# Attention scores from strips of queries and masked keys, without key transfers, in a fused attention and GRU kernel

## What is computed

```python
# x: [128, 32, 256], cond: [128, 256], 16 heads of 16 features
scale, shift = split(cond @ W_emb + b_emb)
xn = rms_norm(x, g_norm) * (1 + scale) + shift
q, k, v = split(xn @ W_qkv)                  # per head
q, k = rms_norm(q, g_q), rms_norm(k, g_k)
attn = softmax(q @ k.T * 16 ** -0.5)         # within one sequence
o = attn @ v
x = x + o + o @ W_out
# GRU cell, for t in range(32), state h starts as cond
gi, gh = x[:, t] @ W_ih + b_ih, h @ W_hh + b_hh
r, z = sigmoid(gi_r + gh_r), sigmoid(gi_z + gh_z)
n = tanh(gi_n + r * gh_n)
h = (1 - z) * n + z * h
x[:, t] = x[:, t] + h
```

## Time and profile before

| what | us |
|---|---|
| median of 3 runs | 341.93 |
| lowest and highest | 341.85, 342.36 |
| span of the profiled execution, first to last instruction | 340.0 |
| TensorE busy in it | 323.3 |
| VectorE, ScalarE, GpSimd busy | 246.3, 238.0, 224.5 |

### The profile page before, as it was taken

The page is one execution under the profiler, slowest core; times in us unless marked ns, Lnnn a source line. Parts: engine busy times, 40 slices in busy tenths (PEclk is TensorE's granted clock), DMA queues, the critical chain, the costliest instruction groups (busy, mean ns, idle before and its releaser), DMA issues.

```text
span 340.0 us, 12168 instructions
## 1 busy us (share of the span) xinstructions
PE 323.3 (95%) x4177; PEld 293.4 (86%) x4177; DVE 246.3 (72%) x665; ACT 238.0 (70%) x722; POOL 224.5 (66%) x404
## 2 busy tenths in 40 slices
PE   8988899899999999999986999999999999999994
PEld 8767788788888888888874999999999999999994
DVE  3778898888999999999996455565555556555555
ACT  4787777778888788889656566666666666666662
POOL 6787787867777877878778346555555555555542
PEclk9999999999999999999999999999999999999999
DMA  5965237742343333233332221111112111122221
GB/s 202 307 193 151 86 76 234 226 132 85 109 121 113 101 114 99 86 117 116 112 109 65 80 77 48 61 49 62 62 62 62 48 58 50 62 62 62 63 62 33
DMA packets 32205, 34.14 MB, mean 100 GB/s; under 512 B 5286, under 2 KB 26796, under 8 KB 32172
## 3 DMA queue, kind: packets, MB, share of 16 engines
q1 hardware_dynamic: 25868, 26.10, 25.6%
q10 hardware_dynamic: 6304, 7.61, 7.0%
HBM read 12.46 MB, written 8.39 MB: 61 GB/s over the span
## 4 chain that ended last, share of the span: by engine, by line
PE 78%; POOL 7%; SPq 4%; DMA 4%; issue 3%; DVE 3%; ACT 1%; POOLq 0%; DVEq 0%; ACTq 0%
PE bank L1287 38%; PE bank L1244 19%; PE bank L1400 4%; PE bank L1419 4%; PE bank L1388 4%; DMA operands<-operands 4%; PE bank L1531 3%; SPq L414 2%; POOL operands L485 2%; PE bank L1380 2%; SPq L405 2%; PE bank L1250 2%; PE bank L1371 2%; POOL xn L496 1%; POOL xn_lo L531 1%
## 5 line engine op out<-in xcount | busy, mean ns | idle before, releaser
L1287 PE MATMUL bank<-wih_lo,wo_parts 128*128 128x256 f32 x192 | 56.2, 294 | 0.0
L1287 PE MATMUL bank<-wih_hi,wo_parts 128*128 128x256 f32 x192 | 54.6, 285 | 0.2 <-POOL pair_lo L600 0.2
L1287 PE MATMUL bank<-wih_hi,pair_lo 128*128 128x256 f32 x192 | 52.8, 279 | 0.0
L1287 PE MATMUL bank<-wqkv_hi,hT_hi 128*128 128x256 f32 x192 | 52.5, 292 | 0.0
L611 POOL TENSOR_TENSOR operands<-operands,h 128x128 f32<-128x128 f32 x64 | 29.6, 462 | 34.2 <-ACT operands L932 33.4
L1287 PE MATMUL bank<-wqkv_lo,hT_hi 128*128 128x256 f32 x192 | 49.9, 279 | 0.0
L1187 DVE TENSOR_TENSOR operands<-bank,operands 128x128 f32<-128x128 f32 x64 | 18.6, 291 | 39.3 <-ACT operands L929 39.3
L1244 PE MATMUL bank<-wqkv_hi,xn_hi 128*128 128x512 f32 (+1 forms) x124 | 46.4, 375 | 0.2 <-POOL xn_lo L531 0.2
L618 POOL TENSOR_TENSOR w_emb_sb<-h,w_emb_sb 128x256 f32<-128x256 f32 x31 | 22.9, 737 | 30.7 <-DVE h L1204 30.7
L1287 PE MATMUL bank<-wqkv_hi,hT_lo 128*128 128x256 f32 x192 | 42.7, 279 | 0.0
L1244 PE MATMUL bank<-wqkv_hi,xn_lo 128*128 128x512 f32 (+1 forms) x124 | 41.9, 338 | 0.0
(11 more groups left out here) (138 smaller groups left out, 975.2 us busy)
## 6 DMA issues: line engine op xcount, KB each, us to landing
v_diag<-v_rows SPq DMA_DIRECT2D x124, 34.0 KB, 2.1
operands<-operands SPq DMA_DIRECT2D x32, 128.0 KB, 2.1
out_dram<-x ACTq DMA_DIRECT2D x16, 256.0 KB, 2.6
w_emb_sb<-out_dram SPq DMA_DIRECT2D x32, 128.0 KB, 2.1
operands<-operands SPq DMA_DIRECT2D x63, 64.0 KB, 2.0
out_dram<-w_emb_sb SPq DMA_DIRECT2D x31, 128.0 KB, 1.7
x_in<-in_x_dram SPq DMA_DIRECT2D x7, 512.0 KB, 8.6
stage_w<-in_L_cond_W_ih_dram ACTq DMA_DIRECT2D x2, 384.0 KB, 3.4
```

The source lines that it names most:

```text
L1287: return pe.matmul(dst, moved, gate_columns(weights, k, block), start=False, stop=True, skip_group_check=True)
```

## The change

The zeros move from the keys to the queries. ScalarE now copies the keys alone (`kT`, 256 columns) and writes the queries twice with a scale per partition (`strip_parity`), which is one for the partitions of every other strip and zero for the rest (`q_strips`, two copies of 256 columns). A product takes 64 partitions of one of these copies as weights and streams the two masked keys of one sequence, 64 columns; there are 32 of them for a group. The scores read `k_masked` directly: `k_diag`, its memset and its transfers are gone, and with them the helpers by which ScalarE's queue took a share of the transfers. With the transfer gone the scores and all that follows have a lag one smaller (`PE_S` 7 to 6 and so on, `POOL_KEYS` stays at 6), GpSimd does `mask_keys` before `shift`, and the extra work of the last turns stands one turn earlier in the program where it is tied to the pipeline's end, on GpSimd for example.

```diff
-PE_X2T, PE_V, PE_S, PE_PV, PE_QKT, PE_OUT, PE_XT, PE_QK = 11, 4, 7, 8, 5, 10, 2, 3
-ACT_LN, ACT_V, ACT_X2T, ACT_QKT, ACT_EXP, ACT_SQX, ACT_SQK, ACT_OT, ACT_XN, ACT_XHAT = 1, 4, 11, 5, 7, 0, 3, 9, 2, 1
-DVE_QKN, DVE_SS, DVE_OT, DVE_MAX, DVE_RCP, DVE_XMOD, DVE_RES, DVE_O, DVE_PT = 4, 3, 8, 6, 7, 1, 9, 7, 6
-POOL_XN, POOL_KEYS, POOL_OT, POOL_XLO, POOL_NEWTON = 3, 6, 10, 3, 1
-SP_V, SP_KEYS = 5, 6
+PE_X2T, PE_V, PE_S, PE_PV, PE_QKT, PE_OUT, PE_XT, PE_QK = 10, 4, 6, 7, 5, 9, 2, 3
+ACT_LN, ACT_V, ACT_X2T, ACT_QKT, ACT_EXP, ACT_SQX, ACT_SQK, ACT_OT, ACT_XN, ACT_XHAT = 1, 4, 10, 5, 6, 0, 3, 8, 2, 1
+DVE_QKN, DVE_SS, DVE_OT, DVE_MAX, DVE_RCP, DVE_XMOD, DVE_RES, DVE_O, DVE_PT = 4, 3, 7, 5, 6, 1, 8, 6, 5
+POOL_XN, POOL_KEYS, POOL_OT, POOL_XLO, POOL_NEWTON = 3, 6, 9, 3, 1
+SP_V = 5
...
             def place_values(v, slot):
                 sp.wait_ge(v_ready, v + 1)
-                for b in range(2 if isinstance(v, int) and v in SHARED_VALUES else GB):
+                for b in range(GB):
...
-            def place_keys(g, slot):
-                sp.wait_ge(k_masked_ready, g + 1)
-                strips = KEY_STRIPS[:-1] if isinstance(g, int) and g == NG - 1 else KEY_STRIPS
-                for i, (first, count) in enumerate(strips):
-                    rows = slice(PB * first, PB * (first + count))
-                    sp.dma_start(k_diag[rows, slot, i % 2, :, :, :].rearrange("p r j k -> p (r j k)"),
-                                 k_masked[rows, slot, :, :].rearrange("p r f -> p (r f)"))\
-                      .then_inc(k_diag_ready[slot], 16)
...
             def mask_keys(k, slot):
-                pool.wait_ge(qkT_ready, k + 1)
+                pool.wait_ge(kT_ready, k + 1)
                 if later(k, 2):
-                    pool.wait_ge(k_diag_ready[slot], spread(k - 2, slot, len(KEY_STRIPS)))
+                    pool.wait_ge(s_ps, k - 1)
...
             def body(base, u):
+                k = group(base, u, POOL_KEYS)
+                if k is not None:
+                    mask_keys(k, (u - POOL_KEYS) % 2)
                 g = group(base, u, POOL_XN)
                 if g is not None:
                     shift(g, (u - POOL_XN) % 2)
-                k = group(base, u, POOL_KEYS)
-                if k is not None:
-                    mask_keys(k, (u - POOL_KEYS) % 2)
...
-                if turn_is(base, u, NG + 5):
+                if turn_is(base, u, NG + 4):
                     summed_biases()
                 for i in range(2 * KC):
-                    if turn_is(base, u, NG + (1, 5, 6, 6)[i]):
+                    if turn_is(base, u, NG + (1, 4, 5, 5)[i]):
                         gate_weights(i // 2, i % 2)
-                    if turn_is(base, u, NG + (5, 6, 7, 7)[i]):
+                    if turn_is(base, u, NG + (4, 5, 6, 6)[i]):
                         state_weights(i // 2, i % 2)
...
-                act.copy(qkT[:, slot, :], p_qkT[:, :]).then_inc(qkT_ready, 1)
+                act.copy(kT[:, slot, :], p_qkT[:, D:2 * D]).then_inc(kT_ready, 1)
+                if isinstance(g, int) and g == 0:
+                    act.wait_ge(parity_step, 4)
+                for n in range(2):
+                    last = act.activation(q_strips[:, slot, n, :], p_qkT[:, 0:D], ACT.Copy,
+                                          scale=strip_parity[:, n:n + 1])
+                last.then_inc(q_strips_ready, 1)
...
-            dve.memset(operands[:, 0:KD], 0.0).then_inc(k_diag_clear, 1)
...
+            dve.tensor_reduce(strip_rows[:, :], head_rows[:, :].rearrange("p (s r) -> p s r", r=2),
+                              AX_X, ALU.add).then_inc(parity_step, 1)
+            dve.wait_ge(parity_step, 3)
+            dve.tensor_reduce(strip_parity[:, :], strip_rows[:, :].rearrange("p (i n) -> p n i", n=2),
+                              AX_X, ALU.add).then_inc(parity_step, 1)
...
             def scores(g, slot):
-                pe.wait_ge(k_diag_ready[slot], spread(g, slot, len(KEY_STRIPS)))
+                pe.wait_ge(k_masked_ready, g + 1)
+                pe.wait_ge(q_strips_ready, g + 1)
...
                 for c in range(KC):
-                    for b in range(GB):
-                        for i in range(2):
-                            rows = slice(2 * PB * i, 2 * PB * i + 2 * PB)
-                            last = pe.matmul(s_tiles[i][T * b:T * b + T, c * P:c * P + P]
-                                             .rearrange("p (r n k) -> p n r k", r=2, k=T),
-                                             qkT[rows, slot, c * P + T * b:c * P + T * b + T],
-                                             k_diag[rows, slot, :, :, GB * c + b, :], start=True, stop=True)
+                    for n in range(2):
+                        for b in range(GB):
+                            tokens = slice(c * P + T * b, c * P + T * b + T)
+                            columns = slice((2 * c + n) * 2 * T, (2 * c + n) * 2 * T + 2 * T)
+                            for i in range(2):
+                                rows = slice(2 * PB * i, 2 * PB * i + 2 * PB)
+                                last = pe.matmul(s_tiles[i][T * b:T * b + T, columns].rearrange("p (r k) -> p r k", r=2),
+                                                 q_strips[rows, slot, n, tokens], k_masked[rows, slot, :, tokens],
+                                                 start=True, stop=True)
```

More of the change, by code:

```diff
@@ L50 @@
 GATE_LOADS = 11
-LATE_RESULTS = range(24, 28)
-LAST_TURNS = range(34, 39)
-SHARED_VALUES = (3, 4)
+LATE_RESULTS = range(25, 29)
+LAST_TURNS = range(33, 38)
 FIRST_SPREAD = 7
@@ L126, in adaptive_attention_gru @@
         qkn = sb("qkn", [P, 2, 2 * D])
[L127 to L134, removed]
+        kT = sb("kT", [P, 2, D])
+        q_strips = sb("q_strips", [P, 2, 2, D])
+        strip_parity = sb("strip_parity", [P, 2])
+        strip_rows = sb("strip_rows", [P, NB])
+        operands = sb("operands", [P, 6 * D])
+        k_masked = operands[:, 0:2 * 2 * D].rearrange("p (s r f) -> p s r f", s=2, r=2)
         v_rows = sb("v_rows", [P, 4, HEADS, VW])
@@ L239, in adaptive_attention_gru @@
         qkT_ps = sem("qkT_ps")
-        qkT_ready = sem("qkT_ready")
+        kT_ready = sem("kT_ready")
+        q_strips_ready = sem("q_strips_ready")
         k_masked_ready = sem("k_masked_ready")
-        k_diag_ready = [sem("k_diag_ready0"), sem("k_diag_ready1")]
         scores_clear = sem("scores_clear")
@@ L407, in place_values @@
                       .then_inc(v_diag_ready[slot], 16)
-            def place_keys(g, slot):
-                sp.wait_ge(k_masked_ready, g + 1)
-                strips = KEY_STRIPS[:-1] if isinstance(g, int) and g == NG - 1 else KEY_STRIPS
-                for i, (first, count) in enumerate(strips):
-                    rows = slice(PB * first, PB * (first + count))
-                    sp.dma_start(k_diag[rows, slot, i % 2, :, :, :].rearrange("p r j k -> p (r j k)"),
-                                 k_masked[rows, slot, :, :].rearrange("p r f -> p (r f)"))\
-                      .then_inc(k_diag_ready[slot], 16)
-            def body(base, u):
[L419 to L426, removed]
+            def body(base, u):
                 v = group(base, u, SP_V)
-                if v is not None and not (isinstance(v, int) and (v <= 2 or v >= NG - 3)):
+                if v is not None:
                     place_values(v, (u - SP_V) % 4)
[L430 to L433, removed]
+                if turn_is(base, u, SP_V + 2):
                     load_x(4 * FIRST_SPREAD, NG, x_loaded[FIRST_SPREAD])
-            pipeline(sp, body, NG - 1 + max(SP_V, SP_KEYS))
+            pipeline(sp, body, NG - 1 + SP_V)
             for stored in x2_stored:
@@ L485, in mask_keys @@
                 pool.tensor_tensor(k_masked[:, slot, :, :],
-                                   qkT[:, slot, D:2 * D].unsqueeze(1).broadcast_to([P, 2, D]),
+                                   kT[:, slot, :].unsqueeze(1).broadcast_to([P, 2, D]),
                                    gqk_parity[:, :].unsqueeze(2).broadcast_to([P, 2, D]),
@@ L692, in load_gate_weights @@
                 act.dma_start(staged[:, i % KC, :], source[(i % KC) * P:(i % KC) * P + P, :]).then_inc(loaded[i % KC], 16)
[L694 to L704, removed]
-                first, count = KEY_STRIPS[-1]
-                rows, slot = slice(PB * first, PB * (first + count)), (NG - 1) % 2
-                act.dma_start(k_diag[rows, slot, (len(KEY_STRIPS) - 1) % 2, :, :, :].rearrange("p r j k -> p (r j k)"),
-                              k_masked[rows, slot, :, :].rearrange("p r f -> p (r f)")).then_inc(k_diag_ready[slot], 16)
             def gate_weights(c):
@@ L897, in body @@
                     first_state()
-                for v in SHARED_VALUES:
-                    if turn_is(base, u, v + ACT_V):
-                        place_values(v, 2, GB)
                 for i in range(4):
@@ L1415, in attention_products @@
                         head = HC * c + 2 * j + e
```

(2 more changed lines are left out.)

17 lines of the change are left out of this document (5 added, 12 removed).

## The result

The changed kernel takes 347.65 us (median of 4 runs, 347.45 to 349.34) against 341.99 us for the kernel before beside it (median of 4). The ratio is 1.017, with an interval of 1.014 to 1.020: 1.7% slower, where the forecast was 340.8 us, and outside its range of 338.0 to 343.8. The profiled execution has a span of 345.7 us, 5.6 more than before, and the 1.9 us between span and median are as they were. One run of the kernel before among those of the experiments, 390.76 us at a granted clock of 0.756, was in a slow state of the chip and is not compared.

What follows compares the result with a forecast made beforehand. TensorE's own work was taken to bound the steady turn. Span: 340.0 + 1.5 (head) - 2.1 (middle) + 0.3 (score products) - 0.8 (tail) = 338.9 us; with 1.9 to the median, 340.8 us, range 338.0 to 343.8.

Steps and rivals of the forecast that it cites:

- the term of the score products: Score block on TensorE: 64 records of 64 columns for 32 of 128 add 0.01 us a group, 0.3 in 32.
- array term: Score block on TensorE: eight records of 53 ns per tile plus 0.16 us for tile-shape change, 0.59 us.
- the low bound: Score block: records taken as free of a fixed part, -0.02 us a group, because the 68-column row is nearly the shape.
- rival E: TensorE's array can't take 64 short records in one pass: +0.35 us on 28 groups, +9.8, 350.3 us; chance 0.08.
- Its small price: Score block: a fixed 25 ns in each record, 0.1 us a group, +2.8, 343.6 us; half of the 0.08.
- rival B: The turn is really gained: head catches up, mask(31) is not held; sum -5.8 us, at half 338; chance 0.15.
- The slow middle turns: Turns from 49.60 to 82.01 us: TensorE's waits for key transfers go, -2.1 us.
- ScalarE: Steady turn: a 256-column copy and two scaled strips for one 512 copy, +0.47 us, covered by its wait for TensorE.
- Rival D: ScalarE becomes the steady turn's bound, strips at 0.63 us each: +3 to +4, about 344.3 us; chance 0.12.
- The head: First turns: shorter lag delays `output_weights` and `normalized`(2), query-key products of turn 10 at 43.5 us; +1.5 us.
- The tail: Last turns: mask(31) waits behind GpSimd's extra work and ScalarE's cast, scores(31) at 179.5 instead of 180.56; -0.8 us.
- The bound of -4.5: Last turns, best case: mask(31) waits for nothing, scores(31) at about 176 us; -4.5 us.

Runs made afterwards that it cites:

- the spread order: Changed kernel with GpSimd's side work of the last turns spread, one or two pieces per turn behind mask(31): 342.61 us, ratio 1.000.
- the mask(31) experiment: Changed kernel with GpSimd's summed biases and weights' low parts of turns 36 and 37 one turn later, behind mask(31): 347.40 us, ratio 1.015.

## Why the prediction was wrong

**The step that failed** is the term of the score products: "I add 0.01 us a group, 0.3 us in 32." It measured 0.19 us a block and 0.20 us a turn, some 6 us in 32 groups, out of 6.8 between the forecast span and the measured one. The prediction's array term was right: eight records of 53 ns on each tile and 0.16 us for the change of shape make 0.59 us, and two blocks of 32 do run at that pace. Its sentence "It must issue eight records in 53 ns; eight start within 0.06 us now" was wrong as a proof. Eight starts show that eight records lay ready, not that 64 can follow at this rate. The first 33 weight loads do. The next seven take from 0.20 to 0.39 us, where 7 x 6.7 ns would be 0.05, and the last 24 come at 8 to 9 ns instead of 6.7: some 0.15 us for the pause and 0.05 us for the pace behind it, which is the whole loss. The kernel before could not show this limit: its block has only 32 records, and the 0.40 us from its first to its last start is close to what the array needs for 128 columns on eight tiles (3 x 107 ns, and the last eight starts). The row of 68 columns, for which the low bound was taken, is also only 32 records long, at 19 ns each (0.61 / 32). Both rows were near in shape and far in the one quantity that decided, records in a row. The case was named, as rival E, with 0.08. Its price of 0.35 a group took all 64 records at 12.6 ns, which was the array's time for 128 columns and not a rate of supply; that the second half of the new block averages nearly the same is chance. Its small price, 0.1 us a group and 343.6 us in all, was too low.

The Trainium skill (TensorEngine Tiling (Array Packing), Instruction Overhead) states some 60 cycles of overhead for a matmul. Neither reading of it gives this: as a floor it makes the split free, and as a part added to each record it makes 0.1 us by the prediction's estimate from that page, also in two halves, where the traces show next to nothing for blocks of 32 records and one pause in a block of 64. The Trainium skill also gives TensorE's queue a depth of 64 (TensorE: Matmul & The Clock Gate, the table of the engine at its start). A record comes with a weight load, which makes two instructions, so 64 of them would be 32 records, and the pause stands behind 33 weight loads. No run here varied that; it is a reading that fits, not one that was shown. What makes the pause stays open.

Two smaller things in the prediction don't follow from its rows. The "about 2 ns per record" that the row of 68 columns is said to leave isn't in them: with 0.16 us for the change of shape its eight records take what their columns take, 57 ns each. And half of rival B's -5.8 us gives 339.0, not 338.

**The slow middle turns**, -2.1 us: right. No wait is left between turns 10 and 34.

**ScalarE**: right. Strips in the steady turn:

```profile
106.97 0.37 ACT L739 COPY kT<-bank 128x256 f32<-128x256 f32 x1
107.24 0.84 ACT L743 ACTIVATE q_strips<-bank,strip_parity 128x256 f32<-128x256 f32 x2
107.96 0.64 ACT L749 ACTIVATE logits<-logits 128x512 f32<-128x512 f32 x1
...
109.31 0.60 ACT L769 ACTIVATE square_qk<-bank 128x512 f32<-128x512 f32 x1 [0.31 <-PE bank L1205]
```

0.27 us for the keys and 0.72 for two strips, 0.36 each where 0.37 was taken, and ScalarE still waits 0.31 us for TensorE. Rival D is excluded.

**The head**, +1.5 us: it was +2.3. The mechanism was right, as far as it was tested. QKT(2) start at 28.59 (28.0 was worked out), directly behind `normalized`(2), which had waited for `output_weights` on VectorE:

```profile
26.83 1.10 DVE L989 TENSOR_TENSOR wo_parts<-stage_wo,wo_parts 128x512 fp32r<-128x512 f32 x1
27.86 0.68 DVE L996 TENSOR_TENSOR qkn<-bank,rs 128x512 f32<-128x512 f32 x1
```
```profile
28.59 0.66 PE L1349 MATMUL bank<-ident,qkn 128*128 128x128 f32 x4 [1.50 <-DVE qkn L996]
```

The query-key products of turn 10 start at 44.50, where 43.5 was worked out. Moving `output_weights` gave 1.1 us back. If the four score blocks up to there lie on the chain in full, their 4 x 0.19 are 0.8 of the 2.3 and the rest is the forecast 1.5; that split is worked out, not tested.

**The tail**, -0.8 us: it was +1.4. The mechanism was right: mask(31) behind the extra work, which waits for the cast; a wait of about 4 us (4.39). Three things were missing. Four longer score blocks (29, 30 and 31 in full, and the one that begins the stretch) are 0.8 us. The clock that falls while TensorE waits costs 1.3 us: the prediction forecasts the wait of 4 us and never asks what TensorE's clock does in it. The third is the rest of 0.1 us, which no run explains. The bound of -4.5 "if mask(31) waited for nothing" is about what the spread order gives: scores(31) start 12.8 us behind the scores of turn 34 there, where the bound's stamp of about 176 is 13.1 behind 162.91.

**The GRU steps**: 0.9 us shorter between the two traces, where the prediction has nothing. In the other kernels with the new layout they take 147.4 to 148.0 us and 148.4 in the experiment that keeps the old layout, so some of the 0.9 may go with the layout. The cause stays open.

By terms, from the forecast span of 338.9 to the measured 345.7: +4.7 from the score blocks of the 24 steady turns, +0.8 from the head, +2.2 from the tail, -0.9 from the GRU steps.

Not tried: a block with more or fewer than 64 records in one piece, which would show where the pause stands and whether it comes again, and score products in another arrangement of tiles. In a block of 64 the step from the first half (c = 0) to the second stands behind record 32, one record ahead of the pause. In the kernel before it stands behind record 16 and the block takes 0.60 us all the same, which speaks against that step as the cause but doesn't exclude it.

## What to carry to other kernels

Splitting matmuls into more and shorter ones has a price of its own that one record or eight starts don't show: count the records in a row and ask for a row of the trace with as many at that pace. Where a pipeline loses a turn, each piece of extra work that stands at its end must be placed anew: two or so at a time between the critical instructions, since the same pieces in front of the mask cost 5.5 us, and in one heap behind it 4.5, against the same pieces spread over the turns. Where a wait of several microseconds of TensorE is left or made, price the clock behind it too.

## What was unexpected of the hardware

A block of 64 short records has a pause in it: 33 weight loads start in 0.20 us, seven in the next 0.19, and the rest at 8 to 9 ns each, the same with strips from ScalarE and with keys from transfers, while blocks of 32 have none. A change of tile shape is dear for such blocks: two halves take 0.77 us in all where their records need 0.43. And behind a single wait of 4.4 us the granted clock was at half level for the next 4.8 us of TensorE's work (185.24 to 190), with the PV block at 1.06 us instead of 0.61. In the mask(31) experiment it was at half level behind a wait of 2.65 us too.
